# All low halves of x for the masked scores made by VectorE, between the residual additions

## The reference

```python
# layers 0, 2 (grouped): 16 heads of 32, 4 key heads
xn = rmsnorm(x, norm_w)
q = xn @ wq; k = cond @ wk; v = cond @ wv
x = x + softmax(q k^T / sqrt(32)) v @ wo
# layers 1, 3 (masked): 16 heads of 64
logits = (x @ Wq) (ctx @ Wk)^T / 8 + col_bias(mask_A, mask_B, token_indices)
x = softmax(logits) (ctx @ Wv) @ Wo + bo + x
```

## Time and profile before

| | us |
|---|---|
| runs of the kernel before | 1622.69, 1622.84, 1625.60 |
| median of them | 1622.84 |
| the profiled execution | 1622.62 |
| span of its trace | 1620.8 |
| TensorE's matmuls busy | 1576.1 |
| VectorE busy | 1092.8 |
| GpSimd busy | 885.4 |
| ScalarE busy | 766.2 |

### The profile page before, as it was taken

One profiled execution on the slowest core, in us unless ns is written; L12 is line 12 of the kernel. 1 busy time (PEld: TensorE's weight loads), 2 busy tenths in 40 slices (PEclk: granted clock), 3 DMA queues, 4 the chain that ended last, 5 costly groups with the idle time before them and its releaser, 6 DMA issues.

```text
span 1620.8 us, 22823 instructions
## 1 busy us (share of the span) xinstructions
PE 1576.1 (97%) x8160; PEld 1330.6 (82%) x8160; DVE 1092.8 (67%) x1825; ACT 766.2 (47%) x1353; POOL 885.4 (55%) x809
## 2 busy tenths in 40 slices
PE   8999999999999999999999999999999999999998
PEld 7998987878878887878787887888787888888787
DVE  6677658766676668756876567665865577656764
ACT  4566656334633465335633463345533554255431
POOL 0532356556754676457655575467645765457531
PEclk9999999999999999999999999999999999999999
DMA  9999562122311331122312232133112231222101
GB/s 337 317 327 372 194 225 75 44 65 98 104 59 33 130 111 41 38 92 85 98 46 65 92 111 59 33 130 111 40 39 82 85 101 53 66 92 85 53 1 52
DMA packets 118431, 171.92 MB, mean 106 GB/s; under 512 B 35760, under 2 KB 69040, under 8 KB 112176
## 3 DMA queue, kind: packets, MB, share of 16 engines
q1 hardware_dynamic: 115424, 153.16, 28.9%
q10 hardware_dynamic: 2736, 16.78, 2.6%
q0 software_dynamic: 160, 0.53, 0.1%
HBM read 118.53 MB, written 51.91 MB: 105 GB/s over the span
## 4 chain that ended last, share of the span: by engine, by line
PE 80%; DVE 13%; issue 4%; DMA 1%; POOL 1%; ACT 1%; SPq 0%; DVEq 0%; POOLq 0%; ACTq 0%
PE OB L364 15%; PE OB L366 14%; PE OB L365 14%; PE SB L364 7%; PE SB L366 7%; PE SB L365 7%; PE TB L481 4%; DVE x L1045 2%; PE MX L364 2%; PE MX L366 2%; PE MX L365 2%; DVE pT L916 2%; PE MX L481 2%; DVE small L1019 1%; DVE prob L1015 1%
## 5 line engine op out<-in xcount | busy, mean ns | idle before, releaser
L1240 POOL TENSOR_TENSOR prob<-prob,small 128x512 f32<-128x512 f32 x256 | 277.3, 1087 | 331.1 <-DVE small L1034 331.1
L777 ACT ACTIVATE pT<-TB 128x512 fp32r<-128x512 f32 x192 | 113.7, 592 | 260.2 <-PE TB L481 260.2
L1234 POOL TENSOR_TENSOR prob<-prob,small 128x512 f32<-128x512 f32 x128 | 136.3, 1065 | 160.3 <-DVE small L1009 160.3
L1015 DVE SCALAR_TENSOR_TENSOR prob<-SB,aux 128x512 f32<-128x512 f32 x128 | 87.9, 686 | 185.4 <-PE SB L366 185.4
L364 PE MATMUL OB<-pT,foldN 128*128 128x512 f32 x512 | 205.0, 400 | 1.0 <-DVE pT L916 1.0
L364 PE MATMUL SB<-foldM,xhl 128*128 128x512 f32 x512 | 201.0, 393 | 4.0 <-issue 3.7
L916 DVE TENSOR_TENSOR pT<-TB,pT 128x512 fp32r<-128x512 f32 x192 | 127.1, 662 | 108.6 <-ACT pT L777 108.6
L365 PE MATMUL OB<-pT,foldN 128*128 128x512 f32 x512 | 199.9, 390 | 0.0
L366 PE MATMUL OB<-pT,foldN 128*128 128x512 f32 x512 | 199.9, 390 | 0.0
L366 PE MATMUL SB<-foldM,xhl 128*128 128x512 f32 x512 | 199.7, 390 | 0.0
L365 PE MATMUL SB<-foldM,xhl 128*128 128x512 f32 x512 | 199.4, 389 | 0.0
(11 more groups left out here) (159 smaller groups left out, 4109.6 us busy)
## 6 DMA issues: line engine op xcount, KB each, us to landing
prob<-in_wkvM_dram SPq DMA_DIRECT2D x32, 512.0 KB, 6.6
ring<-s_fm SPq DMA_DIRECT2D x64, 256.0 KB, 5.2
ring<-s_fn SPq DMA_DIRECT2D x64, 256.0 KB, 2.6
out_dram<-x ACTq DMA_DIRECT2D x15, 1024.0 KB, 3.9
s_fm<-prob SPq DMA_DIRECT2D x32, 256.0 KB, 5.1
wraw<-in_wqG_dram SPq DMA_DIRECT2D x8, 1024.0 KB, 8.5
s_fn<-x SPq DMA_DIRECT2D x32, 256.0 KB, 4.9
ring<-in_xT_dram SPq DMA_DIRECT2D x32, 256.0 KB, 3.4
```

What stands on the lines that cost most here:

```text
L777: act.activation(pT[:, t % 2, 0, :], t_bank(ph, t)[:, :], ACT.Copy).then_inc(S["pt_hi"], 1)
L1015: dve.scalar_tensor_tensor(out=own, in0=bank, scalar=M_SCALE, in1=row, op0=ALU.mult, op1=ALU.add).then_inc(S["biased"], 1)
L1234: pool.tensor_tensor(own, own, hmax[u % 2].unsqueeze(2).broadcast_to([P, HH, KEYS]), ALU.subtract).then_inc(S["evac"], 1)
L1240: pool.tensor_tensor(own, own, rsum[u % 2].unsqueeze(2).broadcast_to([P, HH, KEYS]), ALU.mult).then_inc(S["normed"], 1)
```

## The change

GpSimd makes no low half of x any more. VectorE makes all four at each junction. `xnew` and `xb_lo` take the chunk as an argument, and a new function `xnew_halves` calls them so that a low half stands between two additions: addition 0, addition 1, low 0, addition 2, low 1, addition 3, low 2, low 3. The two semaphores become one, `xb_lo`, on which TensorE counts the chunks in order. At the other two phases' ends the additions stay four in a row. Nothing is changed on ScalarE, SyncE or in the data.

```diff
--- before.py
+++ after.py
...
-                 "exped hsummed summed normed trans prodd pt_hi pt_lo mixed ot_hi ot_lo outd xnew xb_hi xb_lo_p xb_lo_d "
+                 "exped hsummed summed normed trans prodd pt_hi pt_lo mixed ot_hi ot_lo outd xnew xb_hi xb_lo "
...
@@ TensorE, scores()
-                            pe.wait_ge(S["xb_lo_d" if c % 2 else "xb_lo_p"], 2 * e + c // 2 + 1)
+                            pe.wait_ge(S["xb_lo"], 4 * e + c + 1)
...
@@ VectorE
-            def xnew(it, ph):
+            def xnew(it, ph, c):
 
                 k = 4 * it + ph
                 blk = (ph - 1) % 2
-                for c in range(DC):
-                    dve.wait_ge(S["outd"], 4 * (k - 1) + c + 1)
-                    if ph in (1, 2):
-                        if c == 0:
-                            dve.wait_ge(S[f"ld_x{blk}"], 16 * (it + 1))
-                        dve.tensor_tensor(X[blk][:, c, :], OB[c][:, :], X[blk][:, c, :], ALU.add).then_inc(S["xnew"], 1)
-                    else:
-                        dve.scalar_tensor_tensor(out=X[blk][:, c, :], in0=OB[c][:, :], scalar=bout[:, c:c + 1],
-                                                 in1=X[blk][:, c, :], op0=ALU.add, op1=ALU.add).then_inc(S["xnew"], 1)
-
-            def xb_lo(it, ph):
-                for c in (1, 3):
-                    dve.wait_ge(S["xb_hi"], 4 * (2 * it + ph - 1) + c + 1)
-                    lo_part(xhl[:, 1, c, :], X[ph - 1][:, c, :], xhl[:, 0, c, :]).then_inc(S["xb_lo_d"], 1)
+                dve.wait_ge(S["outd"], 4 * (k - 1) + c + 1)
+                if ph in (1, 2):
+                    if c == 0:
+                        dve.wait_ge(S[f"ld_x{blk}"], 16 * (it + 1))
+                    dve.tensor_tensor(X[blk][:, c, :], OB[c][:, :], X[blk][:, c, :], ALU.add).then_inc(S["xnew"], 1)
+                else:
+                    dve.scalar_tensor_tensor(out=X[blk][:, c, :], in0=OB[c][:, :], scalar=bout[:, c:c + 1],
+                                             in1=X[blk][:, c, :], op0=ALU.add, op1=ALU.add).then_inc(S["xnew"], 1)
+
+            def xb_lo(it, ph, c):
+                dve.wait_ge(S["xb_hi"], 4 * (2 * it + ph - 1) + c + 1)
+                lo_part(xhl[:, 1, c, :], X[ph - 1][:, c, :], xhl[:, 0, c, :]).then_inc(S["xb_lo"], 1)
+
+            def xnew_halves(it, ph):
+
+                xnew(it, ph, 0)
+                xnew(it, ph, 1)
+                xb_lo(it, ph, 0)
+                xnew(it, ph, 2)
+                xb_lo(it, ph, 1)
+                xnew(it, ph, 3)
+                xb_lo(it, ph, 2)
+                xb_lo(it, ph, 3)
...
                 pt_lo(it, 2, 0)
-                xnew(it, 1)
-                xb_lo(it, 1)
+                xnew_halves(it, 1)
                 pt_lo(it, 2, 1)
...
                 pt_lo(it, 3, 0)
-                xnew(it, 2)
-                xb_lo(it, 2)
+                xnew_halves(it, 2)
                 sums(it, 2, STEPS - 2, first)
...
@@ GpSimd
-            def xb_lo(it, ph):
-                for c in (0, 2):
-                    pool.wait_ge(S["xb_hi"], 4 * (2 * it + ph - 1) + c + 1)
-                    pool.tensor_tensor(xhl[:, 1, c, :], X[ph - 1][:, c, :], xhl[:, 0, c, :].bitcast(F32),
-                                       ALU.subtract).then_inc(S["xb_lo_p"], 1)
-
...
-                xb_lo(it, 1)
                 norm(it, 1, STEPS - 2)
                 norm(it, 1, STEPS - 1)
...
-                xb_lo(it, 2)
                 norm(it, 2, STEPS - 2)
                 norm(it, 2, STEPS - 1)
```

More of the change, by code:

```diff
@@ L1063, in body @@
                     if not first and u == STEPS - 1:
-                        xnew(it, 0)
+                        for c in range(DC):
+                            xnew(it, 0, c)
                     evac(it, 0, u, first)
@@ L1127, in body @@
                         sums(it, 3, s - 2, first)
-                xnew(it, 3)
+                for c in range(DC):
+                    xnew(it, 3, c)
                 if it == ITS - 1:
@@ L1139, in _ @@
                 pt_lo(ITS, 0, t)
-            xnew(ITS, 0)
+            for c in range(DC):
+                xnew(ITS, 0, c)
         @block.gpsimd
```

## The result

The changed kernel takes 1632.87 us (median of 4 runs, 1631.3 to 1634.5) against 1623.26 for the kernel before (median of 4). The ratio is 1.0057, with a 95% interval of 1.0044 to 1.0069: slower by 0.6%, 9.6 us. The forecast was 1628.1 with a range of 1619.5 to 1633. The direction is right, the measured time lies just inside the range, and the size of the loss was underestimated by almost half.

What follows compares the result with a forecast made beforehand. The prediction took VectorE's queue to close both junctions, with TensorE's matmuls covering 97% of the span. Its sum was 1622.6 + 3.9 (queue waits) + 1.6 (clock) = 1628.1 us, range 1619.5 to 1633.

Steps and rivals of the forecast that it cites:

- VectorE's queue closes the first junction: Phase 1 to 2: gapless VectorE work until 624.70 sets the end; time gained at 617.26 is handed back at 625.52.
- The next job at 5.14: First junction: VectorE's operation after additions and low halves starts 5.14 us behind the first addition, against 4.90, 0.24 later.
- GpSimd's freed time worth 0: Both junctions: GpSimd loses two low halves, 3.00 us per junction, but nothing waits for its time: saving 0.
- The 3.7 us of the earlier trace: TensorE's 8 waits at weight loads for GpSimd's low half of x; priced at 0, as a later wait takes them back.
- Four stretches becoming five: Iteration starts, behind TensorE's 1.9 us wait: one more low-clock stretch, +1.6 us, bounds -6.3 and +4.7.
- TensorE's wait at transpose 3: End of the first junction: the 1.08 us wait at 625.52 for VectorE's transpose low half grows by 0.24.
- Rival (a): Both junctions: only cheaper work counts, -1.6, and scores' stops go, -6.4 at most; 1616 to 1621; chance 0.07.
- part 4: TensorE's scores: first junction ends the same within 0.1, gain 0; second junction has no stop, 0.4 to spare.
- the second step of the reading: Second junction, phase 2 to 3: VectorE's queue closes it, TensorE waiting 0.38 us at 666.95 for a transpose part.
- Part 3: VectorE's queue at both junctions: low halves wait for ScalarE's copies, 0.245 us at each of 16, +3.9 us.
- (b): First junction: GpSimd's low half and VectorE's subtraction, 0.04 us apart, swap order; -9, time about 1617; chance 0.07.
- (e): Slower than forecast: low halves cost 0.845 or a further wait opens; 1633 to 1638; chance 0.08.

Runs made afterwards that it cites:

- the wait of GpSimd: Kernel before plus one wait: GpSimd holds its folded-weight low halves in phase 2 until VectorE's first subtraction is done; 1608.07 us, ratio 0.9912.
- the low halves in a row: Against the kernel before, all four low halves on VectorE, behind the four additions at both junctions; 1620.66 us, ratio 0.9981.
- GpSimd beside VectorE: All low halves on VectorE behind the additions at both junctions, plus two needless GpSimd subtractions at each; 1637.64 us, ratio 1.0090 against the kernel before.
- the one with only its second junction between: Changed kernel with the first junction's four low halves moved behind its four additions; 1629.72 us, ratio 1.0040 against the kernel before.

## Why the prediction was right in its sign and too small

**Right.** VectorE's queue closes the first junction (shown by the wait of GpSimd, 1.12 us straight through). The next job at 5.14 there: measured 5.18, against 4.90 before, and the distance grew by 0.30. At the second junction 5.14 to 5.20: measured 5.24, against 4.95. Low halves of 0.68: median 0.688. One VectorE wait for the last copy: seen at both junctions; the one for the first copy showed at the second junction (0.16) and was below what the view prints at the first. GpSimd's freed time worth 0: it waits 427.0 us for sums where it waited 331.1. The 3.7 us of the earlier trace rows worth 0: so it was. With the low halves in a row TensorE's stops ahead of the scores are longer still, and the first junction is 0.1 shorter, like VectorE's queue.

**Right by luck, and slightly off.** Four stretches becoming five, +1.6: five in the profiled run, but the prediction had only one slow run of the table to go by, and the later kernels had anything from none to seven. TensorE's wait at transpose 3 was to grow by 0.24 and grew by 0.13 (1.08 to 1.21, in all 10.7 to 11.7); the rest of the 0.29 by which that transpose came later is TensorE's own later work. Rival (a) reaches by its own two terms down to 1614.6 (1622.6 - 1.6 - 6.4), not 1616.

**Wrong.** The step that failed is in part 4, at the second junction: "no stop, with 0.4 to spare". This looked only at when the scores want the low halves. Ahead of the scores TensorE runs the first product of the next phase, and `open_out` (line 484) makes its four banks wait for the residual additions, which drain them. At the first junction the product ahead of the scores writes MX, so no bank of OB is wanted there. These are the first matmuls on the third and fourth bank at the second junction of the kernel before, timeline:

```profile
661.86 0.40 PE L364 MATMUL OB<-pT,foldN 128*128 128x512 f32 x1
...
662.56 0.39 PE L364 MATMUL OB<-pT,foldN 128*128 128x512 f32 x1
```

TensorE takes the two banks at 2.28 and 2.98. The third addition ends at 1.87 (2 x 0.60 + 0.67) and the fourth at 2.47, so the drain was in time with 0.4 and 0.5 us to spare and no wait showed. Between low halves additions 2 and 3 end at 2.73 and 3.93 (663.77 and 664.97, each with 0.68), and TensorE gets the banks at 2.79 and 3.99: 0.51 and 1.01 later than before. The scores begin 1.13 late, of which the wait of 0.38 before MX and the slack around it gave 0.54 back. With that the second step of the reading fell too, that VectorE's queue closes this junction: its next job came only 0.29 later, the MX transposes 0.59, and TensorE has no idle time ahead of them. It was the late additions and TensorE's own work behind them that ended last. The term of the second junction was put at 0.2 to 0.25 and measured 0.60: 8 x 0.35 = 2.8 us missing, and the first junction's 0.30 for 0.245 adds 0.4. With both the sum is 1622.6 + 7.2 + 1.6 = 1631.4, against 1631.3 of the profiled run. The remaining 1.6 up to the median are probably further stretches, for which there is only the mean clock: two of the four runs, 1634.1 and 1634.5, have a lower mean clock (0.994, 0.993) than the other two (0.995).

The mistake is one of method. Part 3 asked what is queued behind the new waits on VectorE and who waits for that, and the answer listed the sums and transposes behind the eight operations. The operations moved *inside* the eight, additions 2 and 3, have readers of their own. One is ScalarE's copy, which was in the sum. The other is TensorE's next product, which needs not the value but the free bank.

**The rivals.** (a) was wrong for the change; the order in a row, which it did not speak of, gave the time of its range (1620.66, -2.6 us). (b) did not happen by itself, as expected, since both operations move together (0.04 ahead before, 0.05 after). Forced by a wait it paid 1.12 us a junction, where 1.1 had been worked out, and 4 to 6.5 us of clock besides. (e), "a further wait opens", is the closest to what took place, though its sum began at 1633.

**Open.** What decides whether the 1.9 us stop lowers the clock in an iteration is not shown; no run changed the stop itself. No run kept VectorE's queue of the change and took away the stops at the banks alone, so the split of the 0.60 into queue and banks rests on the trace and on the kernels in which both change together.

## What to carry to other kernels

When an operation is put between others of a queue, list for each one that gets later both who reads its result and who waits for the place it frees; a stop of TensorE at a bank that is not yet drained is not in the trace of before if the drain was just in time. A wait that an engine shows is worth nothing while a later wait closes the same stretch, so find that last one first and look in its queue. Two operations that collide by a few hundredths of a microsecond on the path that sets the end are a cheaper target than the work itself: one wait on the engine with time to spare gave 0.9% here (0.5 of that at the junction, the rest low-clock stretches), the best order of the low halves 0.2%.

## What the hardware showed that was not expected

The same stop of TensorE, 1.9 us at the start of every iteration but the first, lowered its granted clock in some iterations and not in others: behind the stop that ended at 714.8 us in the kernel before, the granted clock was 0.50 from 716 to 718 (1.2 GHz), and behind the one that ended at 539.6 it was 1.00 (2.4 GHz). Where it fell, it did so 0.05 to 1.5 us behind the end of the stop. How many times it fell changed from kernel to kernel though the stop did not (1.91 to 1.93 us in all twelve traces), and kernels with the same matmuls had from none to seven. In the order of the plain distance, in the profiled runs:

| distance, us | 173.9 | 174.2 | 174.9 to 175.0, three kernels | 175.3 | 175.4 | 175.75 | 175.8 | 176.2 | 177.1 | 177.7 |
|---|---|---|---|---|---|---|---|---|---|---|
| stretches of 7 | 0 | 1 | 3 each | 4 | 4 | 4 | 7 | 5 | 2 | 0 |

Each of these costs 1.56 us. The kernel with the longest iteration (177.7, GpSimd beside VectorE) had none, and the one with only its second junction between, 0.4 shorter than the change, had seven where the change had five. The table is one profiled run for each kernel, and it suggests, but does not show, that the distance decides: 175.75 and 175.8 had four and seven, and other runs of one kernel have lower mean clocks than the profiled one (0.992 against 0.996 at 175.75, 0.995 against 0.999 at 177.7). Two kernels less than 2 us apart per iteration (173.9 and 175.8) differ by seven stretches, 11 us of clock. Such a difference came on top of what the junctions gave: the collision's removal, worth 8.1 us by itself, gave 14.6.
